# A fused attention and feed-forward layer: query copies on VectorE, keys transposed in halves, the last intermediate tile by token halves

## The reference

```python
q, k, v = (xn @ W.T + b).reshape(B, S, 32, 32) for (Wq, bq), (Wk, bk), (Wv, bv)
scores = einsum('bshd,bsgd->bshg', q, k) / sqrt(32)      # heads against heads, within one token
scores = where(scores > 0.001, scores, -inf)
attn   = softmax(scores)
out    = einsum('bshg,bsgd->bshd', attn, v) @ Wo.T + bo
gate, up, down = int4-like integers * scale per group of 128
ffn    = (silu(xn @ gate.T) * (xn @ up.T)) @ down.T      # 3584 intermediate values
return x + out + ffn
```

## Time and profile before

| what | value |
|---|---|
| runs shown | 2073.51 to 2074.03 us, median 2074.03 |
| profiled execution | 2074.31 us, of which span 2072.5 |
| PE busy | 1997.5 us (96% of the span) |
| DVE busy | 1561.4 us (75%) |
| POOL busy | 1348.1 us (65%) |
| ACT busy | 1232.2 us (59%) |
| mean granted clock of PE | 0.991 |

### The profile page before, as it was taken

The page is one execution under the profiler, slowest core; times in us unless marked ns, Lnnn a source line. Parts: engine busy times, 40 slices in busy tenths (PEclk is TensorE's granted clock), DMA queues, the critical chain, the costliest instruction groups (busy, mean ns, idle before and its releaser), DMA issues. The chain is left out here.

```text
span 2072.5 us, 35869 instructions
## 1 busy us (share of the span) xinstructions
PE 1997.5 (96%) x10380; PEld 952.7 (46%) x10380; DVE 1561.4 (75%) x1552; ACT 1232.2 (59%) x1988; POOL 1348.1 (65%) x769
## 2 busy tenths in 40 slices
PE   9999999999998999899999999999999999999986
PEld 5555554554554444334444444444444444444434
DVE  6566667667664300699999999999999999999996
ACT  5577777777774311246666666666665666666652
POOL 1455645545553000069888988888888888898885
PEclk9999999999998999999999999999999999999998
DMA  9576676766767372122122112212221212221226
GB/s 271 133 176 167 157 175 159 164 171 154 173 166 185 92 245 76 32 60 51 46 66 66 46 51 61 71 46 51 53 78 46 51 46 73 58 51 46 63 86 247
DMA packets 397931, 217.95 MB, mean 105 GB/s; under 512 B 335427, under 2 KB 372291, under 8 KB 395846
## 3 DMA queue, kind: packets, MB, share of 16 engines
q1 hardware_dynamic: 397894, 217.46, 39.8%
HBM read 94.73 MB, written 41.94 MB: 66 GB/s over the span
## 5 line engine op out<-in xcount | busy, mean ns | idle before, releaser
L1237 POOL TENSOR_TENSOR acc<-acc,lower 128x1024 f32<-128x1024 f32 x327 | 770.4, 2365 | 162.3 <-ACT lower L950 162.2
L655 PE MATMUL banks<-xt,lower 128*128 128x512 f16 x3584 | 857.1, 379 | 13.5 <-DVE lower L1127 8.7
L950 ACT ACTIVATE lower<-banks,down_scale 128x512 f32<-128x512 f32 x654 | 414.4, 684 | 381.4 <-PE banks L680 295.9
L1127 DVE SCALAR_TENSOR_TENSOR lower<-banks,gate_scale,lower 128x1024 f32<-128x1024 f32 x392 | 479.0, 1278 | 143.4 <-PE banks L655 142.4
L655 PEld LDWEIGHTS banks<-xt,lower 128*128 128x128 f16 x3584 | 343.4, 98 | 458.2 <-DVE lower L1127 74.2
L505 PE MATMUL banks<-wt,xt_tile 128*128 128x512 f16 x2304 | 527.9, 379 | 0.0
L1127 DVE SCALAR_TENSOR_TENSOR lower<-banks,up_scale,lower 128x1024 f32<-128x1024 f32 x392 | 479.2, 1278 | 26.6 <-PE banks L655 23.6
L680 PE MATMUL banks<-lower 128*128 (+1 forms) x1792 | 462.3, 382 | 12.0 <-DVE acc L1180 11.8
L1199 POOL TENSOR_TENSOR stacks<-unit,stacks 128x512 f16<-128x512 f32 x192 | 246.8, 1309 | 295.1 <-ACT stacks L779 295.1
L505 PEld LDWEIGHTS banks<-wt,xt_tile 128*128 (+1 forms) x2304 | 218.4, 98 | 229.9 <-issue 1.1
L680 PEld LDWEIGHTS banks<-lower 128*128 (+1 forms) x1792 | 172.5, 98 | 230.7 <-issue 13.0
(11 more groups left out here) (64 smaller groups left out, 1228.5 us busy)
## 6 DMA issues: line engine op xcount, KB each, us to landing
v_scratch<-stacks SPq DMA_DIRECT2D x16, 1024.0 KB, 3.9
lower<-in_L_ffn_gate_q_dram SPq DMA_DIRECT2D x28, 512.0 KB, 3.6
lower<-in_L_ffn_up_q_dram SPq DMA_DIRECT2D x28, 512.0 KB, 4.4
lower<-in_L_ffn_down_q_dram SPq DMA_DIRECT2D x28, 512.0 KB, 3.9
x_tile<-in_L_attn_x_dram SPq DMA_DIRECT2D x16, 512.0 KB, 3.5
xt_scratch<-xt_tile SPq DMA_DIRECT2D x16, 512.0 KB, 2.9
ctx_scratch<-ctx_parts SPq DMA_DIRECT2D x64, 128.0 KB, 2.1
lower<-ctx_scratch SPq DMA_DIRECT2D x4, 2048.0 KB, 8.8
```

Of the source, the lines that this page charges most:

```text
L655: last = mm(psum[:, 2 * (slot % 3) + c, :], gu_t[:, mat, g, :], xt[:, (2 * half + c) * CT:(2 * half + c + 1) * CT, part, g, :], start=(par ...
L950: run(down_tmp[:, buffer, c * BANK:(c + 1) * BANK], psum[:, 6 + c, :], ACT.Copy, scale=scale)\
L1127: v.scalar_tensor_tensor(out=acc_of[:, half, :], in0=gu_pair(slot % 3), scalar=scale[:, :, :].rearrange("p t k -> p (t k)")[:, bass.ds(t * ...
L1237: g.tensor_tensor(acc[:, half, ho, :], acc[:, half, ho, :], down_tmp[:, buffer, :], ALU.add).then_inc(down_added, 1)
```

## The change

**Query copies.** ACT copies batch 2 only, DVE batches 0, 1 and 3. PE's waits are changed to match: batch 2 waits for DVE's copy of batch 0.

**Keys.** `turn_k` issues two transfers, one for each unit of the keys, the first as soon as the low parts of the first unit are made; each has its own semaphore.

**The last tile.** Its gate and up groups run half by half: gate and up of half 0 in the first 16 places, of half 1 in the last 16 (gate and up by turns). silu of half 0 is in place 13. POOL makes the product (place 20) and low part (place 26) of half 0 within the tile, and those of half 1 in the tail; DVE makes none.

**The tail.** Downs 0 to 7 of tile 27 come first, then downs 8 to 10 of tile 26, then the remaining downs with outputs 0 to 5 between them, one before every second down, then outputs 6 to 15. One down less goes to POOL (d = 3 and 6 go to DVE, 4 to POOL). The first half of x is loaded when the groups of half 0 are done, ahead of the last transpose of down weights in SP's list; the second half after the last group.

```diff
-        k_turned = sem("k_turned")
+        k_turned = [sem(f"k_turned{k}") for k in range(2)]
...
+        LAST_ORDER = [(GATE, g, 0) for g in range(5)] + [(UP, 0, 0)]
+        for g in range(5, KT):
+            LAST_ORDER += [(GATE, g, 0), (UP, g - 4, 0)]
+        LAST_ORDER += [(UP, g, 0) for g in range(4, KT)]
+        for g in range(KT):
+            LAST_ORDER += [(GATE, g, 1), (UP, g, 1)]
...
-        LEAD = 11
-        TAIL = [(NI - 2, d) for d in range(EARLY, 16)] + [(NI - 1, d) for d in range(LEAD)]
-        for d in range(LEAD, 16):
-            TAIL += [(OUT, d - LEAD), (NI - 1, d)]
-        TAIL += [(OUT, u) for u in range(16 - LEAD, TT)]
+        HALF_OUT, LAST_OUT = 3, 6
+        TAIL = [(NI - 1, d) for d in range(8)] + [(NI - 2, d) for d in range(8, 8 + HALF_OUT)]
+        for n, item in enumerate([(NI - 2, d) for d in range(8 + HALF_OUT, 16)] + [(NI - 1, d) for d in range(8, 16)]):
+            if n % 2 == 0 and n // 2 < LAST_OUT:
+                TAIL.append((OUT, n // 2))
+            TAIL.append(item)
+        TAIL += [(OUT, u) for u in range(LAST_OUT, TT)]
 
         def by_pool(item):
-            return item[1] % 3 == 1 if item[0] == OUT else item[1] in (1, 3, 6, 9, 11, 14)
+            return item[1] % 3 == 1 if item[0] == OUT else item[1] in (1, 4, 9, 11, 14)
...
-        SILU_AT = {19: 0, 27: 1}
+        OWN_AT = {20: "h", 26: "l"}
+        OWN_HI_AT = 23
...
+        def silu_at(t):
+
+            return {13: 0, 31: 1} if by_halves(t) else {19: 0, 27: 1}
...
-                wait_pos(pe, batch_out[m % 2], j * 2 + m // 2)
+                if m < 2:
+                    wait_pos(pe, batch_out[m], j * (1, 3)[m])
+                else:
+                    pe.wait_ge(batch_out[1], j * 3 + (m - 1))
...
-                        elif kind == "R" and n % 2 == 0:
+                        elif kind == "R" and n == 2:
                             batch_copy(i, n)
...
-                        elif kind == "R" and n % 2:
+                        elif kind == "R" and n != 2:
                             batch_copy(i, n)
...
-            hidden(NI - 1, 0)
-            hidden(NI - 1, 1)
-
-            dve.wait_ge(down_added, 2 + TAIL_FROM)
             for n, (t, d) in enumerate(TAIL_FAST):
-                if n in (0, 2):
-                    hidden_lo(NI - 1, n // 2)
+                if n == 2:
+
+                    dve.wait_ge(down_added, 2 + TAIL_FROM)
...
+                    if idx in OWN_AT and by_halves(t):
+                        (hidden if OWN_AT[idx] == "h" else hidden_lo)(t, 0)
...
+                if n == 2:
+                    hidden(NI - 1, 1)
+                if n == 3:
+                    hidden_lo(NI - 1, 1)
...
-                sp.dma_start_transpose(k_turns, stacks[:, K, :, :].rearrange("p x c -> p (x c)"))\
-                    .then_inc(k_turned, 16)
+                for half in range(2):
+                    sp.wait_ge(unit_lo, i * 6 + (2 * K + 1 + half))
+                    anchor(sp)
+                    at = slice(half * (NH // 2), (half + 1) * (NH // 2))
+                    sp.dma_start_transpose(k_turns[:, at, :], stacks[:, K, at, :].rearrange("p x c -> p (x c)"))\
+                        .then_inc(k_turned[half], 16)
...
-            turn_q(DOWN, NI - 1)
-
-            sp.wait_ge(gu_done, units_made(NI, -1))
+
             for c in range(4):
+                if c == 2:
+                    turn_q(DOWN, NI - 1)
+                if c % 2 == 0:
+
+                    sp.wait_ge(gu_done, units_made(NI - 1, GU_SLOT[15 + 8 * c]))
```

More of the change, by code:

```diff
@@ L397, in in_use, with by_halves, unit_of, index_of @@
             return kind == "gu" or not isinstance(t, int) or t >= 2 or (t == 1 and unit >= FIRST_DOWN)
-        def is_first(slot):
+        LAST_ORDER = [(GATE, g, 0) for g in range(5)] + [(UP, 0, 0)]
[4 more added lines that the diff above has]
+            LAST_ORDER += [(GATE, g, 1), (UP, g, 1)]
+        def by_halves(t):
+            return isinstance(t, int) and t == NI - 1
+        def unit_of(t, idx):
+            if by_halves(t):
+                return LAST_ORDER[idx]
+            return idx // 16, idx // 2 % 8, idx % 2
+        def index_of(t, mat, g, half):
+            return LAST_ORDER.index((mat, g, half)) if by_halves(t) else 16 * mat + 2 * g + half
+        def is_first(t, slot):
             kind, unit = SLOTS[slot]
-            return kind == "gu" and unit // 2 % 8 == 0
+            return kind == "gu" and unit_of(t, unit)[1] == 0
+        def firsts_made(t, mat, half):
+            return t * 4 + ((2 * half + mat if by_halves(t) else 2 * mat + half) + 1)
         def units_made(t, slot):
@@ L410, in adds_made @@
             before = (0, 28)[t] if isinstance(t, int) and t < 2 else 32 * t - 6
-            return before + sum(in_use(t, n) and not is_first(n) for n in range(slot + 1))
+            return before + sum(in_use(t, n) and not is_first(t, n) for n in range(slot + 1))
         def has_prev(t):
@@ L639, in pair_free @@
                     before -= 3
-                if is_first(before):
-                    unit = SLOTS[before][1]
-                    pe.wait_ge(gu_first, tile_of * 4 + (2 * (unit // 16) + unit % 2 + 1))
+                if is_first(tile_of, before):
+                    mat, _, half = unit_of(tile_of, SLOTS[before][1])
+                    pe.wait_ge(gu_first, firsts_made(tile_of, mat, half))
                 else:
@@ L922, in first_group @@
                 anchor(act)
-                run(acc_of[:, half, :], gu_pair(GU_SLOT[16 * mat + half] % 3), ACT.Copy,
+                run(acc_of[:, half, :], gu_pair(slot % 3), ACT.Copy,
                     scale=scale[:, :, :].rearrange("p t k -> p (t k)")[:, bass.ds(t * KT, 1)]).then_inc(gu_first, 1)
             def silu(t, half):
-                act.wait_ge(gu_added, adds_made(t, GU_SLOT[14 + half]))
+                act.wait_ge(gu_added, adds_made(t, GU_SLOT[index_of(t, GATE, KT - 1, half)]))
                 wait_pos(act, h_lo, t * 2 + (half - 1))
@@ L954, in tile @@
                 for idx in range(32):
-                    if idx in (0, 1, 16, 17):
-                        first_group(t, idx // 16, idx % 2)
+                    mat, g, half = unit_of(t, idx)
+                    if g == 0:
+                        first_group(t, mat, half)
                     for back, d in downs(t, idx):
@@ L963, in tile @@
                         hidden_hi(t - 1, int(idx == HI_AT1))
-                    if idx in SILU_AT:
-                        silu(t, SILU_AT[idx])
+                    if idx in silu_at(t):
+                        silu(t, silu_at(t)[idx])
+                    if idx == OWN_HI_AT and by_halves(t):
+                        hidden_hi(t, 0)
                     if idx == CONV_GATE and has_next(t):
@@ L1109, in first_tile @@
                 opening(weights, lambda: x_part(0), first_quarter, second_x)
-                batch_copy(0, 1)
-                batch_copy(0, 3)
+                for m in (0, 1, 3):
+                    batch_copy(0, m)
             walk(dve, first_tile, tile_2)
```

42 lines of the change are left out of this document (17 added, 25 removed).

## The result

The changed kernel takes 2038.94 us (median of 6 runs, 2037.63 to 2040.64); the kernel before took 2074.03 in 6 runs beside it (2073.38 to 2074.89). The ratio is 0.9831, 95% interval [0.982, 0.9841]: 35.1 us faster, against 32.8 predicted. The profiled execution took 2038.04 us with a span of 2036.2, so in the traces the gain is 2072.5 - 2036.2 = 36.3 us. A second set of runs gave 2038.21.

The account below looks back on a forecast made before the run. TensorE (PE) was taken as the bound, busy 1997.5 of 2072.5 us. Gains of 16.1 + 0.3 + 2.6 + 13.8 = 32.8 us off 2074.31 gave 2041.5, with the median 0.28 lower 2041.2; range 2032 to 2050.

Parts of the forecast that it names:

- What bounds the kernel: Whole kernel: PE is the bound; a change wins only where PE idles or runs below full clock.
- Part 1, the copies: Attention: moving query copies to DVE removes PE's wait for ACT; 16.1 us over 13 steady tiles.
- The ring: Steady attention tiles: head products, softmax and probabilities' transposes form a loop of 36.80 us that sets the step.
- The rival (a): Attention loop loose or POOL's tail quicker: PE gets the whole 1.42 us per tile; 2037 us, chance 0.15.
- Tile 0: First attention tile: PE waits for two successive DVE copies instead; 0.3 us won, between 0 and 2.0.
- Part 2, the keys: Keys' transpose in halves: 0 in steady tiles, Wo's transfers start and end earlier; 2.6 us won.
- the upper bound of 4.9: Wo stage: most the halved keys could win, if all PE's waits for Wo rows went; 4.9 us.
- under 1 us: Sign at Wo: PE's wait near 665 us falls to under 1 us.
- Part 3, the last tile and the tail: End of kernel: waits of 11.8 us go, clock stays up, POOL's list sets the end; 13.8 us won.
- The rival (c): Tail gives about half: idle gaps let PE's clock fall or POOL's queue is longer; 2048 us, chance 0.2.
- (b): Attention: POOL held up by DVE's new copy, 0.9 us more per tile; 2053 us, chance 0.05.
- (d): Keys' transpose priced by the instruction, each half costing like a whole: slower than before, 2083 with 5.5; chance 0.02.

Follow-up runs that it names:

- x_moved: Changed kernel with the split of the next x behind the exponentials and SyncE's list reordered to probabilities, keys, then x: 2044.83 us, ratio 0.9861.
- pool_less: Changed kernel with down 11 of tiles 26 and 27 added by DVE, taken from POOL's list: 2036.21 us, ratio 0.9824.
- x_between: Changed kernel with the x split behind the exponentials, x's transpose between the second and third of the probabilities', keys last: 2040.46 us, ratio 0.9839.
- pool_less_alt: Changed kernel with down 11 of tiles 26 and 27 on DVE and the last tile's up groups starting after three gate groups: 2036.86 us, ratio 0.9819.

## Why the prediction was right, and where its terms were off

**What bounds the kernel**: right. Nothing came from the 1273 us between Wo and the last tile, in which PE hardly idles; all came from attention, Wo and the stretch behind the last groups.

**Part 1, the copies.** The ring was to take 36.80 us and PE to wait some 0.2 at product 0. The traces have 36.87 and 0.25, and 13 steps bring 15.4 of the 16.1 us. Of the difference, 0.1 us is the start of product 0 after the landing, which the sum left out. The rival (a), a loose ring, would have had steps of 36.62 us and no wait at product 0. Tile 0 was off: 0.3 taken, 1.8 found. The waits there are only 0.45 us shorter, as expected. The remaining 1.3 us are the clock. In the kernel before it fell in tile 0, behind 1.98 us of waiting; in the changed kernel PE waits in two pieces and it did not fall. Whether the change keeps it up is open: in the keys-only kernel, with the long wait, it did not fall either (last section).

**Part 2, the keys.** The mechanism was right (one row of transfers, started earlier, ends as much earlier), and 0 in the steady tiles was right. The size was not: 2.6 against 4.7 in the trace and 4.1 to 5.5 between the kernels with and without it. The term that was mis-sized is the start of the row: it was to be 2.4 to 2.6 us earlier and is 3.1 against the kernel before (the loads of Wo at 13.68 and 10.60 us behind the probabilities' issue), and PE's last wait ends 3.4 earlier. The term that was left out is the clock behind that wait, 1.3 us. The result lies near the upper bound of 4.9 without being what that bound stood for: PE still waits, 2.17 us where "under 1 us" was said.

In the steady tiles the halves do not land 2.4 us earlier, as the prediction has it. SP's queue holds the probabilities until 286.99, so the first half goes at 288.05 and not when POOL has its operands ready; the two take 3.07 and 2.11 us, and SP is through 8.47 us after product 0 (284.95 to 293.42), against 8.52 before (292.61 to 301.13). It cost nothing, because the scores had slack either way.

**Part 3, the last tile and the tail.** All steps hold. POOL's list up to its last down was counted as 33.0 us from the end of the groups (2041.6 - 2008.57) and takes 32.6; output 8 waits for it; the clock doesn't fall; the last group ends 48.3 us before the end (47 to 51 were named). The last tile is 1.1 us longer (1.0 taken), with two waits for DVE of together 0.54 us among it. The net is 14.6 us against 13.8. The rival (c), a tail that gives half, did not come: PE's gaps of 1.3 us between outputs did not let the clock fall while it had work (to 2027.8).

**(b)**, POOL held by DVE's new copy, did not come either. POOL's eight operations on the probabilities start at 316.89, beside DVE's copy of 316.50 to 317.71, and take 5.08 us, against 5.07 before. The copy reads PSUM. The Trainium skill (SBUF — State Buffer, Who interferes with whom) says that an instruction of VectorE with at most one SBUF input, outside the two-port modes, does not contend with GpSimd; the trace agrees. **(d)**: both halves together take 5.37 us of queue time in the steady tile, against 4.86 for the whole, so a half does not cost what a whole one does.

The sum was 3.5 us too small on the span. The terms of tile 0 and Wo make 3.6 of it, of which some 2.6 are the clock; attention and the last stretch miss by 0.7 and 0.9 in opposite directions, so that part of the agreement is luck.

## What to carry to other kernels

When a wait goes, close the ring: add the times from the operation that waits next around to itself, and the gain is the smaller of the wait and the ring's slack. Of a step that is moved, follow each transfer that depends on it through the issuing queue: a transpose that waits in the middle of SP's list holds everything behind it, and that cost more (10.6 us) than the ring had to give (3.3). In a tail that is bound by an engine other than the busiest one, count that engine's list operation by operation; here it was right to 0.5 us of 33.

## What the runs showed of the hardware

**The clock after the same wait.** The kernel before and the keys-only kernel have the same matmuls and copies in tile 0 and the same wait; only the keys' transposes differ. In the profile of before the clock fell behind it and six matmuls took 2.60 us; in the other it did not and they took 1.46. From 72 to 80 us the mean granted clock was 0.79 in the one and 1.00 in the other.

```profile
74.18 1.63 PE L518 MATMUL banks<-ident,stacks 128*128 128x128 f16 x16 [1.98 <-ACT turned L785]
75.60 2.60 PE L505 MATMUL banks<-wt,xt_tile 128*128 128x512 f16 x6
```

```profile
74.27 1.07 PE L518 MATMUL banks<-ident,stacks 128*128 128x128 f16 x16 [1.99 <-ACT turned L786]
75.17 1.46 PE L505 MATMUL banks<-wt,xt_tile 128*128 128x512 f16 x6
```

At the first probabilities' issue that is 1.4 us (97.72 and 96.36). What decides is open. The tail-only kernel, whose tile 0 is that of the kernel before, fell like it (0.79 from 72 to 80 us); the DMA engines also did less in the keys-only kernel then (a share of 0.52 against 0.79). But one kernel can end either way, it seems: of the tail-only kernel's four runs three had a mean clock of 0.995 and took 2059.8 to 2060.9 us, the fourth 0.998 and 2056.57; where in the kernel is not known. So a wait of 2 us cost 2 or some 3.4 us here, and a term with such a wait in it needs that as its range.

**An operation with two SBUF inputs beside POOL.** DVE's L1041 subtracts one SBUF operand from another. In the changed kernel it runs beside POOL's L1225 and takes 2.18 us, while POOL's two operations take 4.20; moved behind the exponentials, where POOL is idle for all but the last 0.2 us of it, it takes 1.21, and the same pair on POOL takes 2.27 elsewhere in the changed kernel (293.16). First the changed kernel, then x_moved:

```profile
307.49 4.20 POOL L1225 TENSOR_TENSOR stacks<-unit,stacks 128x512 f16<-128x512 f32 x2 [6.84 <-ACT stacks L815]
...
308.49 2.18 DVE L1041 TENSOR_TENSOR x_parts<-x_tile,x_parts 128x1024 f16<-128x1024 f32 x1
```

```profile
318.05 1.21 DVE L1041 TENSOR_TENSOR x_parts<-x_tile,x_parts 128x1024 f16<-128x1024 f32 x1
```

The Trainium skill (SBUF — State Buffer, Who interferes with whom) says that an instruction of VectorE with two SBUF inputs contends with one of GpSimd that reads SBUF. The trace agrees: L1041 loses 1.0 us and POOL's pair 1.9. Not all of the latter is due to L1041: L1076, which has two SBUF inputs as well, lies beside the same pair, and with L1041 moved away (x_moved, 310.62) the pair still takes 3.22 us beside L1076 and L1080.

**A longer wait need not mean later data.** The wait for Wo's rows was 2.17, 2.63, 4.69 and 5.26 us in four kernels (the changed one, pool_less, x_between, pool_less_alt) that up to there are the same, but for the place of x in the third. The rows are there at nearly the same time in all of them, 16.5 to 17.1 us after PE's first transposes of Wo. What differs is when PE comes to wait: from 628 to 637 us the mean granted clock was 0.66 to 0.67 where the wait was short and 1.00 where it was long. The price comes behind the wait: to the third group of output matmuls PE then took 7.1 us in the first two and 8.8 in the last two, where the clock fell. Over the thirteen traces of this case it stayed up in five, with waits of 2.1 to 3.3 us, and fell in eight, with waits of 2.9 to 5.3; the wait alone does not decide it.
